# Two bias additions move from GpSimd instructions to accumulating transfers that GpSimd issues

## The chip, the cores and the metric

The kernel runs on one core of one Trainium2 chip. The metric is the device time of one execution in microseconds (us), where less is better. The engines are named as the profile names them: PE is the matrix engine (PEld is its loading of weights), DVE the vector engine, ACT the scalar engine, POOL GpSimd, and SP the engine whose queue issues most transfers between DRAM and the on-chip memory.

## The reference, cut to what matters

```python
x = layernorm(x + attn(x))        # linear attention, 16 heads
x = layernorm(x + xattn(x, ctx))  # channel attention, two variants added, 4 heads
x = layernorm(x + ffn(x))         # one expert of 8 for each batch

def attn(x):
    q, k, v = split(x @ Wqkv.T + bqkv)
    q, k = elu(q * scale) + 1, elu(k * scale) + 1
    y = q * cumsum(k * v) / max(sum(q * cumsum(k)), 0.001)
    return y @ Wproj.T + bproj                 # bproj: 512 numbers

def ffn(x):
    e = argmax(x.mean(1) @ Wr + br)            # for each batch
    return relu(x @ W1[e] + b1[e]) @ W2[e] + b2[e]   # b2[e]: 512 numbers
```

x and ctx are 16 batches of 512 tokens by 512 channels in fp32. The change touches how the two biases at the ends of these functions, `bproj` and `b2[e]`, come into x.

## The kernel before, in words

Every matrix product is done three times with operands split into a high part (rounded to fp32r) and a low part (the rest): high by high, high by low, low by high. ACT rounds (`wq`, `xT_hi`, `we_hi`, `h_hi`), DVE subtracts to get the low part (`xT_lo`, `we_lo`, `h_lo`).

The kernel is a software pipeline written out by hand. An outer loop runs over i = 0 to 19, an inner one over h = 0 to 31. In step i five stages work on five batches: a = i (attention), c = i-1 (channel attention), e = i-2 (second normalisation and choice of the expert), b = i-3 (the expert's two products) and z = i-4 (third normalisation and the store). In each h, a function `mix(i, h)` of each engine emits what the stages a, c, e and z have at this h; between these pieces stand the products of the expert's layers, `up` at even h and `down` at odd h. The four compute engines and SP have one program each, in this order, and meet at semaphores (`dve.wait_ge(proj_mm, ...)`). An engine runs its own instructions in order, so what stands behind a waiting instruction waits with it.

Names that are needed below:

- `X[n]`, n = 0 to 3, are four buffers of 128 partitions by 4x512 fp32 (1 MB). Batch a is in `X[a % 4]` from its load (`x_tok`, SP, at h = 15) to its store four steps later. Everything is added to it in place.
- POOL adds `bproj` to `X[a]` (L338 in the kernel before) after the load has landed (`xtok_in`), from a copy of the bias on all partitions, `rows[:, BPROJ]`. It signals `xb_done`. DVE's `residual1(a, t)` (L643) waits for that and for the projection's product, at h = 24 to 27.
- POOL adds `b2` to `X[b]` (L320) at the head of step i, after PE has transposed x (`tr_mm`), from a small tile `b2` that SP has loaded for the chosen expert (L254). It signals `b2_done`; DVE's `residual3(z, t)` (L658) waits for it one step later, at h = 1.
- Behind L320 on POOL stands `diagonal(c_col)` (L311), which PE's `ctx_sums` (L951) needs at h = 5. Behind L338 stands `diagonal(k_all2)` (L311), which waits for DVE (`kall2_done`, L735) and which PE's `constants` (L992) needs at h = 21.
- DVE's `weigh(c, v)` at h = 16 and 17 turns the exponentials into weights (`junk_v` L722, `a_v` L726, their sum L738). PE's `attention_T` (L985) transposes the sum at h = 19. DVE's `denominator(a)` at h = 18 (L605 to L611) leads over ACT (`rden_all`, L506) to PE's `spread_reciprocal` (L916) at h = 20.
- SP loads the expert's weights into two buffers `raw` (L260), each as soon as DVE has made the low part of the chunk two before (`wlo_done`, L760); ACT rounds a chunk at L424. It loads the projection weights `wq` for q, k and v again in each step (L191) into three buffers.

Of the kernel before, what the change touches and what calls it, by code (L numbers as in the profile page):

```python
# [7 lines left out]
ALU = mybir.AluOpType  # L8
# [3 lines left out]
P = 128  # L12
NB = 16
T = 512
C = 512
CC = C // P
TT = T // P
# [5 lines left out]
NE = 8  # L23
# [11 lines left out]
NX = 4  # L35
# [17 lines left out]
def build(nc, d, out):  # L53
    wq_dram = nc.dram_tensor("wq_scratch", [JOBS, P, 2 * CC * P], F32, kind="Internal").ap()

    with ExitStack() as ctx:
        def sb(name, shape, dt=F32):
            return ctx.enter_context(nc.sbuf_tensor(name, shape, dt))

        def sem(name):  # L60
            return ctx.enter_context(nc.semaphore(name))
# [18 lines left out]
        ctx_T = sb("ctx_T", [P, CC, T])  # L80
        e_f, r_f = sb("e_f", [P, T]), sb("r_f", [P, T])
        k_sum, kv_sum, q = sb("k_sum", [P, T]), sb("kv_sum", [P, T]), sb("q", [P, T])
        rows = sb("rows", [P, 9, C])
        WKG, BKG, WKL, BKL, WVG, BVG, WVL, BVL, BPROJ = range(9)
        c_sb = sb("c_sb", [P, XH, P])
        diag = sb("diag", [P, XH, P])
        s_a, a_v = sb("s_a", [P, 2, XH, P]), sb("a_v", [P, 2, XH, P])
        aT = sb("aT", [P, XH, P])
        const_b = sb("const_b", [P, C])
        x_sum = sb("x_sum", [P, C])  # L90
        b2 = sb("b2", [P, 1, C])

        ident, ones = sb("ident", [P, P]), sb("ones", [P, P])
        head_sum = sb("head_sum", [P, CC, SEG])
# [64 lines left out]
            sem(n) for n in ("mean_mm", "mcol_done", "route_mm", "logit_done", "top_done", "found_done", "idx_done"))  # L159
        tr_mm, x2hi_done, x2lo_done = sem("tr_mm"), sem("x2hi_done"), sem("x2lo_done")  # L160
        we_in = [sem(f"we_in{s}") for s in range(NR)]
        b1_in, b2_in = [sem("b1_in0"), sem("b1_in1")], sem("b2_in")
        whi_done, wlo_done = sem("whi_done"), sem("wlo_done")
        up_mm, h_done, hhi_done, hlo_done, down_mm, acc_mm = (
            sem(n) for n in ("up_mm", "h_done", "hhi_done", "hlo_done", "down_mm", "acc_mm"))
        b2_done, res3_done, stored = sem("b2_done"), sem("res3_done"), sem("stored")
        JOB_MM = (k_mm, v_mm, q_mm)

        block = ctx.enter_context(nc.Block())
# [5 lines left out]
        def _(sp):  # L175
# [21 lines left out]
            sp.dma_start(b_qkv[:, :], d["b_qkv"]).then_inc(small_in, 16)  # L197
            sp.dma_start(scale[:, :], d["scale"].broadcast_to([P, 1])).then_inc(small_in, 16)
            load_raw(3)
            sp.dma_start(rows[:, :, :], d["rows"].broadcast_to([P, 9, C])).then_inc(consts_in, 16)  # L200
            sp.dma_start(wr[:, :, :], d["wr"]).then_inc(consts_in, 16)
            sp.dma_start(br[:, :], d["br"]).then_inc(consts_in, 16)
            sp.dma_start(X[NX - 1][:, :, :].rearrange("p t n -> p (t n)"), d["w_proj"]).then_inc(wp_in, 16)
# [1 line left out]
            for i in range(NB + 4):  # L205
                a, c, e, b, z = stages(i)
                for h in range(HALVES):
                    if h in JOB_AT:
                        j = JOB_AT.index(h)
                        if i == 0:  # L210
                            store_job(j)
                            if j + 4 < JOBS:
                                load_raw(j + 4)
                        if i > 0 and inside(a) and j + NQ < JOBS:
                            load_job(a, j + NQ)
                        if inside(a + 1) and j + NQ >= JOBS:
                            load_job(a + 1, j + NQ - JOBS)
                    if h == 11 and inside(z):
                        sp.wait_ge(norm_done, TT * z + TT)
                        sp.dma_start(out[z], X[z % NX][:, :, :]).then_inc(stored, 16)  # L220
                    if h == 15 and inside(a):

                        if (due := upto(z, 16, 16)) is not None:
                            sp.wait_ge(stored, due)
                        if a == NX - 1:
                            sp.wait_ge(wplo_done, 1)
                        sp.dma_start(X[a % NX][:, :, :], d["x_tok"][a]).then_inc(xtok_in, 16)
                    if h == 18 and inside(a + 1):

                        sp.wait_ge(den_mm, a + 1)  # L230
                        sp.dma_start(xT_raw[:, :, :], d["xT"][a + 1]).then_inc(xT_in, 16)
                    if h == 23 and inside(a):

                        sp.wait_ge(yhi_done, CC * a + CC)
                        sp.wait_ge(ylo_done, CC * a + CC)
                        sp.dma_start(ctx_tok[:, :, :], d["ctx_tok"][a]).then_inc(ctx_in, 16)
                    if h == 26 and inside(a):

                        if (due := upto(c, TT, TT)) is not None:
                            sp.wait_ge(out_mm, due)  # L240
                        if (due := upto(c, XH, XH)) is not None:
                            sp.wait_ge(csum_done, due)
                        sp.dma_start(ctx_T[:, :, :], d["ctxT"][a]).then_inc(ctxT_in, 16)
                    if h == 26 and inside(e):
                        sp.wait_ge(idx_done, e + 1)
                        expert = sp.value_load(idx[0:1, e:e + 1], min_val=0, max_val=NE - 1)

                        if (due := upto(e - 2, FC, FC)) is not None:
                            sp.wait_ge(h_done, due)
                        sp.dma_start(b1[:, e % 2, :], d["b1"][bass.ds(expert, 1)].rearrange("a p f -> p (a f)")).then_inc(b1_in[e % 2], 16)  # L250

                        if (due := upto(e - 1, 1, 1)) is not None:
                            sp.wait_ge(b2_done, due)
                        sp.dma_start(b2[:, 0, :], d["b2"][bass.ds(expert, 1), :].broadcast_to([P, C])).then_inc(b2_in, 16)  # L254
                    g = FC * b + h // 2 + 3
                    if h % 2 == 1 and 0 <= g < NB * FC:

                        if g >= NR:
                            sp.wait_ge(wlo_done, g - NR + 1)
                        sp.dma_start(raw[:, g % NR, :],  # L260
                                     d["w12"][bass.ds(expert, 1), g % FC].rearrange("a p n -> p (a n)")).then_inc(we_in[g % NR], 16)
# [3 lines left out]
        def _(pool):  # L265
# [48 lines left out]
            for i in range(NB + 4):  # L314
                a, c, e, b, z = stages(i)
                if inside(b):

                    pool.wait_ge(tr_mm, CC * b + CC)
                    pool.wait_ge(b2_in, 16 * b + 16)
                    pool.tensor_tensor(X[b % NX][:, :, :], X[b % NX][:, :, :],  # L320
                                       b2[:, 0:1, :].broadcast_to([P, TT, C]), ALU.add).then_inc(b2_done, 1)
                if inside(c):
                    pool.wait_ge(csum_done, XH * c + XH)

# [10 lines left out]
                    rstd_of(2, z)  # L335
                if inside(a):
                    pool.wait_ge(xtok_in, 16 * a + 16)
                    pool.tensor_tensor(X[a % NX][:, :, :], X[a % NX][:, :, :],  # L338
                                       rows[:, BPROJ:BPROJ + 1, :].broadcast_to([P, TT, C]), ALU.add).then_inc(xb_done, 1)
                if inside(c):  # L340
                    pool.wait_ge(kall2_done, c + 1)

# [204 lines left out]
        def _(dve):  # L547
# [90 lines left out]

            def residual1(a, t):
                dve.wait_ge(proj_mm, TT * a + t + 1)  # L640
                dve.wait_ge(xb_done, a + 1)
                x = X[a % NX][:, t, :]
                dve.tensor_tensor(x, AB[(t + 1) % 2][:, :], x, ALU.add).then_inc(res1_done, 1)  # L643

# [6 lines left out]
            def residual3(z, t):  # L651
                if t < TT - 1:
                    dve.wait_ge(acc_mm, (TT - 1) * z + t + 1)
                else:
                    dve.wait_ge(down_mm, FC * z + FC)
                dve.wait_ge(b2_done, z + 1)
                x = X[z % NX][:, t, :]
                dve.tensor_tensor(x, acc[t][:, :], x, ALU.add).then_inc(res3_done, 1)  # L658

# [495 lines left out]
```

## Time and profile before

| | us |
|---|---|
| median of 3 runs | 2568.96 (2568.95 to 2569.8) |
| the profiled execution, its own time | 2571.94 |
| its span, first to last instruction | 2570.2 |
| PE busy | 2430.1 (95% of the span) |
| DVE busy | 1747.5 (68%) |
| ACT busy | 1172.2 (46%) |
| POOL busy | 533.6 (21%) |
| transfers, share of 16 DMA engines | 37.4% |

The times are device times; the profile is one more execution, in which every instruction is recorded. A line of the profile names the line of the kernel, the engine, the operation, what is written and what is read, and for an engine that stood idle in front of the instruction, what released it. "Issue" stands where the profile shows nothing that was waited for.

### The profile page before, as it was taken

Reading aid. Unit: us, or ns where it says so; the run is one execution under the profiler, and the core shown is the slowest. Engines: PE = TensorE matmul, PEld = TensorE weight load, DVE = VectorE, ACT = ScalarE, POOL = GpSimd, SP = SyncE. Lnnn points to the kernel's source line nnn. Section 1 sums busy time; section 2 is a strip of 40 time slices with the busy share of each in tenths; the row PEclk is TensorE's granted clock in tenths of the full one; section 3 lists DMA queues with packets and bytes.
Section 4 is the critical chain, followed back from the end, with each engine's and each line's share of the span. In section 5 each row is a group of like instructions: output and inputs, shape, how many; then the busy total and the mean of one; then the engine's idle time right before and its main releaser. Section 6 shows DMA issues by size and latency. Waiting matters only on the chain.

```text
span 2570.2 us, 33240 instructions
## 1 busy us (share of the span) xinstructions
PE 2430.1 (95%) x11584; PEld 1988.8 (77%) x11584; DVE 1747.5 (68%) x2721; ACT 1172.2 (46%) x1920; POOL 533.6 (21%) x452
## 2 busy tenths in 40 slices
PE   6866899999999999999999999999999999999998
PEld 5655688878788787878878787887878888877876
DVE  6567576677767677676767768667776767765443
ACT  4223444545444443554544455454545445354543
POOL 3132212122112212221122122212212221222110
PEclk9877899999999999999999999999999999999999
DMA  7333333433434344343433434343343434222332
GB/s 274 113 109 107 127 141 117 140 136 108 172 103 159 116 139 145 106 156 119 156 119 121 150 124 160 112 146 128 115 158 117 156 114 145 95 82 87 115 108 69
DMA packets 83400, 331.85 MB, mean 129 GB/s; under 512 B 11810, under 2 KB 11810, under 8 KB 72738
## 3 DMA queue, kind: packets, MB, share of 16 engines
q1 hardware_dynamic: 83234, 329.72, 37.4%
q8 instruction: 94, 1.54, 0.2%
q14 instruction: 72, 0.59, 0.1%
HBM read 306.61 MB, written 23.07 MB: 128 GB/s over the span
## 4 chain that ended last, share of the span: by engine, by line
PE 81%; DVE 10%; ACT 4%; issue 3%; DMA 1%; POOL 1%; SPq 0%; ACTq 0%; DVEq 0%; POOLq 0%
PE m L868 25%; PE acc L1045 24%; PE h_ps L868 23%; DVE junk_v L722 3%; PE m L1003 2%; PE m L944 2%; DVE a_v L726 2%; ACT const_b L465 1%; PE m L1019 1%; PE m L916 1%; PE m L951 1%; DVE h_lo L768 1%; POOL diag L311 1%; PE m L992 1%; ACT rden_all L506 1%
## 5 line engine op out<-in xcount | busy, mean ns | idle before, releaser
L868 PE MATMUL m<-xT_hi,wq 128*128 128x512 f32 x1536 | 514.2, 399 | 24.8 <-DVE wq L550 10.7
L424 ACT ACTIVATE we_hi<-raw 128x1024 fp32r<-128x1024 f32 x256 | 270.7, 1058 | 505.4 <-PE acc L1045 500.3
L760 DVE TENSOR_TENSOR we_lo<-raw,we_hi 128x1024 fp32r<-128x1024 f32 x256 | 368.7, 1440 | 177.6 <-ACT we_hi L424 177.6
L1045 PE MATMUL acc<-we_hi,h_hi 128*128 128x512 f32 x1024 | 423.3, 413 | 0.4
L868 PE MATMUL h_ps<-x2T_hi,we_hi 128*128 128x512 f32 x1024 | 403.4, 394 | 6.0 <-DVE x2T_lo L754 6.0
L1045 PE MATMUL acc<-we_hi,h_lo 128*128 128x512 f32 x1024 | 400.8, 391 | 0.0
L1045 PE MATMUL acc<-we_lo,h_hi 128*128 128x512 f32 x1024 | 400.5, 391 | 0.0
L868 PE MATMUL h_ps<-x2T_lo,we_hi 128*128 128x512 f32 x1024 | 399.6, 390 | 0.0
L868 PE MATMUL h_ps<-x2T_hi,we_lo 128*128 128x512 f32 x1024 | 399.6, 390 | 0.0
L434 ACT ACTIVATE hid<-h_ps,b 128x512 f32<-128x512 f32 x256 | 175.7, 686 | 458.5 <-PE h_ps L868 458.5
L868 PEld LDWEIGHTS m<-xT_hi,wq 128*128 128x128 f32 x1536 | 295.2, 192 | 91.1 <-issue 28.0
L768 DVE TENSOR_TENSOR h_lo<-hid,h_hi 128x512 fp32r<-128x512 f32 x256 | 182.9, 714 | 253.1 <-ACT h_hi L439 252.9
L868 PE MATMUL m<-xT_lo,wq 128*128 128x512 f32 x768 | 304.3, 396 | 0.0
L1045 PEld LDWEIGHTS acc<-we_hi,h_hi 128*128 128x128 f32 x1024 | 193.4, 189 | 49.1 <-issue 9.6
L868 PEld LDWEIGHTS h_ps<-x2T_hi,we_hi 128*128 128x128 f32 x1024 | 192.7, 188 | 45.7 <-DVE x2T_lo L754 6.7
L1045 PEld LDWEIGHTS acc<-we_lo,h_hi 128*128 128x128 f32 x1024 | 193.5, 189 | 43.4 <-issue 7.0
L1045 PEld LDWEIGHTS acc<-we_hi,h_lo 128*128 128x128 f32 x1024 | 192.9, 188 | 42.3
L868 PEld LDWEIGHTS h_ps<-x2T_hi,we_lo 128*128 128x128 f32 x1024 | 192.8, 188 | 40.4
L868 PEld LDWEIGHTS h_ps<-x2T_lo,we_hi 128*128 128x128 f32 x1024 | 192.9, 188 | 38.6
L381 ACT ACTIVATE e_f<-m,sb_qkv,scale 128x512 f32<-128x512 f32 x128 | 99.9, 780 | 220.8 <-PE m L868 217.5
L338 POOL TENSOR_TENSOR x<-x,rows 128x2048 f32<-128x2048 f32 x16 | 74.1, 4629 | 544.4 <-DMA x<-in_x_tok 544.4
L868 PEld LDWEIGHTS m<-xT_lo,wq 128*128 128x128 f32 x768 | 147.9, 193 | 31.3 <-issue 1.0
(126 smaller groups left out, 3480.4 us busy)
## 6 DMA issues: line engine op xcount, KB each, us to landing
raw<-in_w SPq DMA_DIRECT2D x256, 512.0 KB, 3.8
wq<-wq_scratch SPq DMA_DIRECT2D x180, 512.0 KB, 3.3
xT_raw<-in_xT SPq DMA_DIRECT2D x16, 1024.0 KB, 5.9
x<-in_x_tok SPq DMA_DIRECT2D x16, 1024.0 KB, 5.4
ctx_tok<-in_ctx_tok SPq DMA_DIRECT2D x16, 1024.0 KB, 4.9
ctx_T<-in_ctxT SPq DMA_DIRECT2D x16, 1024.0 KB, 4.9
out_dram<-x SPq DMA_DIRECT2D x16, 1024.0 KB, 4.8
wq_scratch<-wq SPq DMA_DIRECT2D x12, 512.0 KB, 4.5
```

The costliest lines, as they stand in the source:

```text
L338: pool.tensor_tensor(X[a % NX][:, :, :], X[a % NX][:, :, :], rows[:, BPROJ:BPROJ + 1, :].broadcast_to([P, TT, C]), ALU.add).then_inc(xb_do ...
L381: act.activation(e_f[:, :], ps[:, :], ACT.Exp, bias=sb_qkv[:, col:col + 1], scale=scale[:, 0:1]).then_inc(done, 1)
L424: act.activation(we_hi[:, g % NW, :], raw[:, g % NR, :], ACT.Copy).then_inc(whi_done, 1)
L434: act.activation(hid[:, f % 2, :], H_PS[:, :], ACT.Relu, bias=b1[:, b % 2, f:f + 1]).then_inc(h_done, 1)
L722: dve.scalar_tensor_tensor(junk_v[:, h % 2, :], s_a[:, v, h, :], e_rec2[:, v, h:h + 1], rows[:, bv, h * P:h * P + P], ALU.mult, ALU.mult, ...
L726: dve.scalar_tensor_tensor(a_v[:, v, h, :], s_a[:, v, h, :], e_rec2[:, v, h:h + 1], rows[:, wv, h * P:h * P + P], ALU.mult, ALU.mult).then ...
L760: dve.tensor_tensor(we_lo[:, g % NW, :], raw[:, g % NR, :], we_hi[:, g % NW, :].bitcast(F32), ALU.subtract).then_inc(wlo_done, 1)
L768: dve.tensor_tensor(h_lo[:, f % 2, :], hid[:, f % 2, :], h_hi[:, f % 2, :].bitcast(F32), ALU.subtract).then_inc(hlo_done, 1)
L868: last = pe.matmul(out, lhsT, rhs, start=(n == 0), stop=(n == 3 * len(pairs) - 1))
L944: last = pe.matmul(by_head[:, h, :], X[c % NX][:, t, hs], ctx_tok[:, t, hs], start=(t == 0), stop=(t == TT - 1))
L1003: last = pe.matmul(M2[:, h * P:h * P + P], ctx_T[:, h, t * P:t * P + P], aT[:, h, :], start=True, stop=True)
L1045: last = pe.matmul(acc[t][:, :], hx[:, f % 2, ts], wx[:, g % NW, C:], start=(f == 0 and n == 0), stop=(f == FC - 1 and n == 2))
```

## The change

Both additions leave POOL's arithmetic. In their place POOL issues a transfer from DRAM into `X` that adds what it brings to what is there (`accum_op=ALU.add`). The source is a row of 512 numbers in DRAM, read again for each of 128 partitions and 4 token groups; the destination is the whole 1 MB buffer. Since the row of `b2` depends on the expert, POOL now reads the index itself. The tile `b2`, its load by SP, its semaphore `b2_in` and the ninth row of `rows` go. `b2_done` becomes two semaphores, used in turn, and `xb_done` counts 16 for each batch.

```diff
@@ sp
-                        if (due := upto(e - 1, 1, 1)) is not None:
-                            sp.wait_ge(b2_done, due)
-                        sp.dma_start(b2[:, 0, :], d["b2"][bass.ds(expert, 1), :].broadcast_to([P, C])).then_inc(b2_in, 16)
@@ pool
                 if inside(b):
 
+                    pool.wait_ge(idx_done, b + 1)
+                    expert = pool.value_load(idx[0:1, b:b + 1], min_val=0, max_val=NE - 1)
                     pool.wait_ge(tr_mm, CC * b + CC)
-                    pool.wait_ge(b2_in, 16 * b + 16)
-                    pool.tensor_tensor(X[b % NX][:, :, :], X[b % NX][:, :, :],
-                                       b2[:, 0:1, :].broadcast_to([P, TT, C]), ALU.add).then_inc(b2_done, 1)
+                    pool.dma_start(X[b % NX][:, :, :], d["b2"][bass.ds(expert, 1), :].unsqueeze(1).broadcast_to([P, TT, C]),
+                                   accum_op=ALU.add).then_inc(b2_done[b % 2], 16)
...
                 if inside(a):
                     pool.wait_ge(xtok_in, 16 * a + 16)
-                    pool.tensor_tensor(X[a % NX][:, :, :], X[a % NX][:, :, :],
-                                       rows[:, BPROJ:BPROJ + 1, :].broadcast_to([P, TT, C]), ALU.add).then_inc(xb_done, 1)
+                    pool.dma_start(X[a % NX][:, :, :], d["b_proj"].broadcast_to([P, TT, C]), accum_op=ALU.add).then_inc(xb_done, 16)
@@ dve
             def residual1(a, t):
                 dve.wait_ge(proj_mm, TT * a + t + 1)
-                dve.wait_ge(xb_done, a + 1)
+                dve.wait_ge(xb_done, 16 * a + 16)
...
-                dve.wait_ge(b2_done, z + 1)
+                dve.wait_ge(b2_done[z % 2], 16 * (z // 2) + 16)
```

On POOL, this is one step of the kernel before, from the addition of `b2` (L320) to the one of `bproj` (L338) and the diagonal behind it:

```order
L320 TENSOR_TENSOR x3<-x3,b2 128x2048 [waits b2_in,tr_mm]
L311 TENSOR_TENSOR diag<-ident,c_col 128x512 [waits kb_mm,csum_done]
L305 TENSOR_TENSOR x_sum<-x0 128x512 [waits sx_mm,x2_done]
L308 TENSOR_TENSOR x_sum<-x_sum,x0 128x512 [waits x2sum_done] x2
L295 TENSOR_TENSOR var_e<-mv,ln_eps 128x4 [waits norm_done,mv2_done]
...
L338 TENSOR_TENSOR x2<-x2,rows 128x2048 [waits xtok_in]
L311 TENSOR_TENSOR diag<-ident,k_all2 128x512 [waits c_mm,kall2_done]
```

The same stretch of POOL in the changed kernel (its line numbers are four or five lower) is this:

```order
L314 TENSOR_LOAD idx [waits idx_done]
L314 ISA x2
L316 ISA [waits tr_mm]
L316 DMA x<-in_b 128x4x512
L306 TENSOR_TENSOR diag<-ident,c_col 128x512 [waits kb_mm,csum_done]
L300 TENSOR_TENSOR x_sum<-x 128x512 [waits sx_mm,x2_done]
L303 TENSOR_TENSOR x_sum<-x_sum,x 128x512 [waits x2sum_done] x2
L290 TENSOR_TENSOR var_e<-mv,ln_eps 128x4 [waits norm_done,mv2_done]
...
L334 DMA x<-in_b_proj 128x4x512 [waits xtok_in]
L306 TENSOR_TENSOR diag<-ident,k_all 128x512 [waits c_mm,kall2_done]
```

Nothing has changed places: each addition is replaced where it stood, and the first one has the reading of the index in front of it. DVE, ACT and PE keep their instructions and their order; on SP only the load of `b2` is gone.

## Rows read from the trace of the kernel before

**Rows 1.** The page: the busy time of the engines and its share of the span.
```profile
PE 2430.1 (95%) x11584; PEld 1988.8 (77%) x11584; DVE 1747.5 (68%) x2721; ACT 1172.2 (46%) x1920; POOL 533.6 (21%) x452
```
**Rows 2.** Busy time in a stretch: length, PE, PEld, DVE, ACT, POOL, clock, DMA share, GB/s.
```profile
304.00:1131.00 827.00, 813.20 (x3927) 667.92 (x3927) 590.12 (x913) 396.63 (x659) 167.73 (x135) 1.00 0.39 134
```
**Rows 3.** Waits of PE over the run: us in total, times, the longest.
```profile
PE m L868 <- issue: 23.9, 15, 1.6
PE m L985 <- DVE a_v L738: 21.0, 14, 7.7
PE m L916 <- ACT rden_all L506: 11.6, 3, 6.2
```
**Rows 4.** Instructions of DVE's line L722: ns min/median/max, first and last start.
```profile
L722 DVE SCALAR_TENSOR_TENSOR junk_v<-s_a,e_rec,rows x128: 345/349/4744, 136.1 to 2324.8; 128x128 f32<-128x128 f32 x128
```
**Rows 5.** POOL in order of time in one middle step: start, duration, idle before.
```profile
1197.92 5.05 POOL L320 TENSOR_TENSOR x<-x,b 128x2048 f32<-128x2048 f32 x1
1227.09 1.04 POOL L311 TENSOR_TENSOR diag<-ident,c_col 128x512 f32<-128x512 f32 x1 [24.11 <-ACT const_b L465]
...
1281.14 4.59 POOL L338 TENSOR_TENSOR x<-x,rows 128x2048 f32<-128x2048 f32 x1 [34.77 <-DMA x<-in_x_tok]
1290.33 1.08 POOL L311 TENSOR_TENSOR diag<-ident,k_all 128x512 f32<-128x512 f32 x1 [4.60 <-DVE k_all L735]
```
**Rows 6.** DVE in order of time in the same step.
```profile
1199.03 5.03 DVE L760 TENSOR_TENSOR we_lo<-raw,we_hi 128x1024 fp32r<-128x1024 f32 x1
...
1281.23 4.65 DVE L722 SCALAR_TENSOR_TENSOR junk_v<-s_a,e_rec,rows 128x128 f32<-128x128 f32 x1
...
1291.60 0.69 DVE L738 TENSOR_TENSOR a_v<-a_v 128x512 f32<-128x512 f32 x1
...
1314.16 0.67 DVE L643 TENSOR_TENSOR x<-m,x 128x512 f32<-128x512 f32 x1
```
**Rows 7.** PE in order of time around the transposes of h = 19.
```profile
1291.07 0.39 PE L868 MATMUL h_ps<-x2T_hi,we_lo 128*128 128x512 f32 x1
1292.34 0.66 PE L985 MATMUL m<-ident,a_v 128*128 128x128 f32 x4 [0.88 <-DVE a_v L738]
...
1295.42 0.39 PE L1045 MATMUL acc<-we_lo,h_hi 128*128 128x512 f32 x1
1295.65 0.39 PE L1045 MATMUL acc<-we_hi,h_lo 128*128 128x512 f32 x1
1296.12 0.73 PE L916 MATMUL m<-rden_all,head_all 128*128 128x512 f32 x2
...
1299.88 1.02 PE L992 MATMUL m<-diag,ones 128*128 128x512 f32 x2
```
**Rows 8.** DVE and PE in order of time in the steps i = 1 and 2.
```profile
138.45 4.25 DVE L713 TENSOR_TENSOR e_rec<-e_rec,wp 128x4 f32<-128x4 f32 x1
...
146.68 1.11 PE L985 MATMUL m<-ident,a_v 128*128 128x128 f32 x4 [7.74 <-DVE a_v L738]
...
242.33 3.22 DVE L609 CAST den<-rden 128x128 fp32r<-128x128 f32 x1
...
248.00 1.22 PE L916 MATMUL m<-rden_all,head_all 128*128 128x512 f32 x2 [6.18 <-ACT rden_all L506]
```
**Rows 9.** POOL and DVE in order of time in step i = 0.
```profile
59.55 4.55 POOL L338 TENSOR_TENSOR x<-x,rows 128x2048 f32<-128x2048 f32 x1 [40.36 <-DMA x<-in_x_tok]
...
71.80 0.69 DVE L643 TENSOR_TENSOR x<-m,x 128x512 f32<-128x512 f32 x1 [5.34 <-PE m L868]
```
**Rows 10.** Transfers by kind (KB each, median us to landing), and SP and ACT in time.
```profile
raw<-in_w SPq DMA_DIRECT2D x256, 512.0 KB, 3.8
...
x<-in_x_tok SPq DMA_DIRECT2D x16, 1024.0 KB, 5.4
...
1296.03 3.55 SPq L260 DMA_DIRECT2D raw<-in_w  x2
...
1303.77 1.06 ACT L424 ACTIVATE we_hi<-raw 128x1024 fp32r<-128x1024 f32 x1 [1.26 <-PE acc L1045]
```

More of the change, by code:

```diff
@@ L82, in build @@
         k_sum, kv_sum, q = sb("k_sum", [P, T]), sb("kv_sum", [P, T]), sb("q", [P, T])
-        rows = sb("rows", [P, 9, C])
-        WKG, BKG, WKL, BKL, WVG, BVG, WVL, BVL, BPROJ = range(9)
+        rows = sb("rows", [P, 8, C])
+        WKG, BKG, WKL, BKL, WVG, BVG, WVL, BVL = range(8)
         c_sb = sb("c_sb", [P, XH, P])
@@ L90, in build @@
         x_sum = sb("x_sum", [P, C])
-        b2 = sb("b2", [P, 1, C])
         ident, ones = sb("ident", [P, P]), sb("ones", [P, P])
@@ L161, in build @@
         we_in = [sem(f"we_in{s}") for s in range(NR)]
-        b1_in, b2_in = [sem("b1_in0"), sem("b1_in1")], sem("b2_in")
+        b1_in = [sem("b1_in0"), sem("b1_in1")]
         whi_done, wlo_done = sem("whi_done"), sem("wlo_done")
@@ L165, in build @@
             sem(n) for n in ("up_mm", "h_done", "hhi_done", "hlo_done", "down_mm", "acc_mm"))
-        b2_done, res3_done, stored = sem("b2_done"), sem("res3_done"), sem("stored")
+        b2_done, res3_done, stored = [sem("b2_done0"), sem("b2_done1")], sem("res3_done"), sem("stored")
         JOB_MM = (k_mm, v_mm, q_mm)
@@ L199, in _ @@
             load_raw(3)
-            sp.dma_start(rows[:, :, :], d["rows"].broadcast_to([P, 9, C])).then_inc(consts_in, 16)
+            sp.dma_start(rows[:, :, :], d["rows"].broadcast_to([P, 8, C])).then_inc(consts_in, 16)
             sp.dma_start(wr[:, :, :], d["wr"]).then_inc(consts_in, 16)
@@ L1134 @@
         "scale": g["L0_attn_scale"].reshape(1, 1),
-        "rows": np.stack([x_names[n] for n in ("wkg", "bkg", "wkl", "bkl", "wvg", "bvg", "wvl", "bvl")]
-                         + [g["L0_attn_bproj"]])[None],
+        "rows": np.stack([x_names[n] for n in ("wkg", "bkg", "wkl", "bkl", "wvg", "bvg", "wvl", "bvl")])[None],
+        "b_proj": g["L0_attn_bproj"].reshape(1, 1, C),
         "cols": np.stack([column(x_names[n]) for n in ("wqg", "bqg", "wql", "bql", "wp", "bp")], axis=1),
```

## The prediction

> **What bounds the kernel now.** I read the page first, then the busy time by stretches, the waits of PE, and one middle step in order of time on POOL, DVE and PE. The page says PE: busy for 2430.1 us, 95% of the span [rows 1]. From 304 to 1131 us PE is busy for 813.2 of 827 us at full clock [rows 2]: 13.8 us, 1.7%, are without work. So nothing that merely relieves POOL or DVE can bring more than that in the middle of the run, and only where PE's wait ends on the relieved work. The waits of PE name the places [rows 3]: the transposes L985 wait for DVE's a_v for 21.0 us in 14 waits, the first spreading product L916 for 11.6 us, and a third group, ahead of the projection, for 23.9 us in 15.
>
> POOL is busy for 21% of the span and stands idle ahead of most of its work [rows 1, 5], so its own time is worth nothing. What its additions do to DVE is the point. While L338 runs (1281.14 to 1285.73), DVE's L722 takes 4.65 us from 1281.23 to 1285.88; the median of this line is 0.349 us [rows 4 to 6]. It ends when POOL's instruction ends. The same stands at the other addition: L320 runs from 1197.92 to 1202.97, and DVE's we_lo takes 5.03 us beside it [rows 5, 6]. So a big addition on POOL holds up a DVE instruction with two on-chip inputs for its whole length. In steps a = 3 to 14 it is each time the weighing of the attention (I counted 12), and behind it come the sum L738 and the transposes on PE.
>
> **The change part by part.**
>
> *The addition of bproj leaves POOL.* DVE gets 4.65 - 0.35 = 4.3 us back in each middle step. PE uses only what it waits for. The last product before the transposes starts at 1291.07; products follow each other every 0.23 us (1295.42, 1295.65), so the transposes could start at 1291.30 and start at 1292.34: 1.04 us lost. The product L916 could start at 1295.88 and starts at 1296.12: 0.24 us [rows 7]. Both waits end on DVE's chain, which now comes 4.3 us earlier, that is 3.3 and 3.0 us before PE asks. Together 1.28 us a step, twelve times: 15.4 us.
>
> In step 1 DVE's L713, an instruction of four columns, takes 4.25 us beside the addition, against some 0.16 us for such a row elsewhere, and PE waits for 7.74 us on what follows [rows 8]. The whole 4.1 us comes back. In step 2 the held instruction is the cast L609, 3.22 us where its others take 0.23, and PE waits for 6.18 us on rden_all behind it [rows 8]: 3.0 us. As a check, the group of L985 has 21.0 us [rows 3]: 12 x 0.88 in the middle and 7.74 in step 1 leave 2.7, which is step 2's, where a_v was made before the addition began and the wait stays; of the 11.6 us of L916 6.18 are step 2's. The third group, 1.6 us a step ahead of the projection, I count as staying: the addition of const_b (L350), which is not changed, holds DVE there in the same way.
>
> Gain so far: 15.4 + 4.1 + 3.0 = 22.5 us.
>
> *The addition of b2 leaves POOL.* DVE's we_lo gets 3.8 us back, but no wait of PE ends on it: the three groups of [rows 3] stand elsewhere, and PE has other products between h = 0 and 4. Nothing gained. POOL reads the index and issues; the next thing on its queue, the diagonal at 1227.09, sits idle for 24.11 us on ACT [rows 5], so this costs nothing up to that length. The sum in X is wanted by residual3 a step later, over 150 us: the transfer is covered whatever it takes. SP loses one load a step, off the path.
>
> *The transfer that adds bproj, issue.* The trace shows no transfer issued by POOL. Below, SP's issues return within half a microsecond; above, the addition itself, 4.6 us. I take 2 us. Behind it on POOL waits the diagonal of k_all, which ran at 1290.33 to 1291.41 while PE's L992 starts at 1299.88 [rows 5, 7]. With PE 1.3 us earlier POOL may be busy until 1297.5, so an issue of up to 16 us costs nothing.
>
> *The same, landing.* This is the unknown that matters. The nearest row is the plain load of the same megabyte, 5.4 us from issue to landing [rows 10]. An adding transfer must also read the destination: twice, 10.8 us, is my value. As bounds I take 5.4 us and 25 us (POOL's 4.6 us as issue, and four times a load's time, since the row doesn't say what 512 pieces of 2 KB in place of 128 of 8 KB cost). The deadline is residual1: in the middle steps L643 starts at 1314.16, 33.0 us after POOL was free to begin [rows 5, 6]; in steps 1 and 2 it is 28 and 24 us by the same two lines; in step 0 it is 71.80 - 59.55 = 12.25 us [rows 9]. With 10.8 us all hold, step 0 by little, and there the path of its first use is new. I charge 1 us for step 0.
>
> *The same, beside other transfers.* The engines for transfers are in use for 39% of the time [rows 2]. Of the loads that run within 15 us of the issue, the one that is needed soonest is raw at 1296.03, landing 3.8 us later and rounded by ACT at 1303.77 [rows 10]: 3.9 us to spare, as much again as the load itself takes. The load before it was issued only once the held DVE had made its low part, and comes 4 us earlier now. So sharing costs nothing unless the adding transfer is still running at 1296, 15 us after its issue.
>
> Two rules of the Trainium skill, SBUF — State Buffer, section Who interferes with whom, bear on the unseen issue. A DVE instruction with two inputs in SBUF contends with a GpSimd instruction that reads SBUF, not with one that only writes it; by this, writing descriptors would not hold DVE, and all of the 4.3 us returns. Against the change, the same section says that the making of descriptors starves while DVE is in a two-port mode. Whether the cast and the scalar maximum of the denominator run so no row tells; they are 0.23 and 0.28 us long, so by it the transfer starts half a microsecond later at most, and the sum stays. No run here shows either for a transfer.
>
> As an estimate from the formula of DMA: Bandwidth & Descriptors, section Anatomy of one DMA, about 2 us plus the bytes over 436 GB/s, a plain megabyte takes 4.4 us, and with the read counted as well 6.8 us; the rows' 5.4 us for the plain load are the firmer ground.
>
> **The sum.** -22.5 + 1 = -21.5 us. On the profiled execution's own time, 2571.94 us (span 2570.2), that gives 2550.4; on the median of the runs, 3.0 us less than this execution, 2547.5 us, 0.84% faster.
>
> **The rivals.**
>
> *The transfer lands late (slower).* Place: residual1 waits for xb_done, DVE's queue stands, and the two PSUM banks of the projection are not freed. Each us beyond 12 costs step 0 a us, beyond about 21 step 2, beyond 24 step 1, beyond 31.7 (33.0 less PE's gain) all middle steps. At 26 us the cost is 14 + 5 + 2 = 21 us: break even. At 36 us it is 24 + 15 + 12 + 12 x 4.3 = 103, less 22.5: 2649 us. For it: an addition in a transfer is unseen, and each partition's row is read back in 2 KB pieces. Against it: it would have to take five to seven times a plain load. Chance 0.12.
>
> *The middle case, 14 to 24 us.* Step 0 loses 2 to 12 us, and raw at 1296 loses its margin in some steps, up to 0.5 us a step. Gain 5 to 18: 2551 to 2564, say 2556 us. Chance 0.15.
>
> *The issue holds DVE as the addition did.* If POOL's issue lasts and blocks like L338, DVE gets nothing back: 2568 to 2572 us. The hold must be over 3.0 us to cost anything of the middle steps, and 4.3 to cost all. For it: both are work of POOL on the on-chip memory. Against it: the source comes from DRAM, and POOL reads no tile. Chance 0.10.
>
> *More than forecast.* With DVE ahead, the wait before the projection goes as well, 15 x 1.6 = 24 us more: 2524 us. Against it: it hangs on L350, which moves along with PE. Chance 0.03.
>
> **How the numbers follow.** Forecast 0.60, with a range of its own of 2542 to 2554 (from the middle steps alone, 15.4 us, to the full 22.5 and 4 us more in the first 300 us, where PE's clock isn't steadily granted). With the middle case, 0.75; to leave out no more than 2 in 10, the range goes on to the no-change case: 2541 to 2567. A measurement of this kernel tells 0.2%, 5 us, from no change. Faster: 0.60 + 0.03 + 0.13 of the middle case = 0.76. Same: 0.10 + 0.02 = 0.12. Slower: 0.12.
>
> **What the profile of after would show.** Right: no L722, L713 or L609 over 1 us; the group PE m L985 waiting for a_v gone; each middle step of PE 1.3 us shorter; the group ahead of the projection still 1.6 us a step; DVE's we_lo at the head of a step near 1.2 us. The issue on POOL shows as a row or as a gap ahead of the diagonal. Wrong: DVE's x (L638 there) with idle time ended by the transfer x<-in_b_proj, in step 0 first; DVE rows of 4 us beside POOL's issue; ACT's we_hi waiting for raw; or a landing beyond 25 us.

## The result, and the profile after

The changed kernel takes 2537.89 us (median of four runs, 2537.43 to 2539.95), the kernel before 2569.17 us in the same session (2568.95 to 2569.80). The ratio is 0.9878, 95% interval 0.9866 to 0.9890: 1.22%, 31.3 us, faster. The forecast was 2547.5 us, with a range of 2541 to 2567, so the gain was 10 us larger than forecast and 3 us outside the range. The profiled execution took 2537.97 us, its span is 2536.3 us. That is 33.9 us less than the span before, and the accounts below are of these 33.9 us.

The page of after, engines and transfers (KB each, median us from issue to landing):
```profile
PE 2417.4 (95%) x11584; PEld 1987.2 (78%) x11584; DVE 1631.3 (64%) x2721; ACT 1171.4 (46%) x1920; POOL 423.6 (17%) x452
...
q0 software_dynamic: 16896, 33.56, 8.6%
...
raw<-in_w SPq DMA_DIRECT2D x256, 512.0 KB, 4.2
...
x<-in_b_proj POOLq DMA_DIRECT2D x16, 1024.0 KB, 12.2
...
x<-in_b POOLq DMA_DIRECT2D x16, 1024.0 KB, 11.6
```
Two stretches of after, with the columns of [rows 2]:
```profile
304.00:1131.00 827.00, 818.33 (x3991) 675.48 (x3990) 560.84 (x945) 397.05 (x660) 135.58 (x138) 1.00 0.48 149
200.00:230.00 30.00, 23.10 (x115) 18.66 (x115) 24.65 (x42) 11.26 (x29) 4.54 (x3) 0.96 0.46 158
```
and the second of them in the kernel before:
```profile
200.00:230.00 30.00, 25.40 (x104) 19.97 (x105) 22.40 (x36) 8.86 (x21) 5.71 (x4) 0.83 0.32 105
```
In 827 us PE now runs 3991 products in place of 3927 [rows 2], and 8.7 us are without work in place of 13.8. The second stretch shows something else: the granted clock is 0.96 there and was 0.83, and PE finishes eleven products more in a shorter busy time.

The waits of PE after, which answer to [rows 3]:
```profile
PE m L863 <- issue: 23.9, 15, 1.6
...
PE m L911 <- ACT rden_all L501: 7.9, 3, 3.4
PE m L1014 <- DVE x2T_lo L749: 7.7, 1, 7.7
...
PE m L980 <- DVE a_v L733: 6.6, 2, 3.7
```
The group ahead of the projection is the same to the tenth. The transposes wait in steps 1 and 2 alone; the twelve middle waits are gone. One middle step, as in [rows 5 to 7], POOL first:
```profile
1260.35 1.35 POOL L334 DMA_DIRECT2D x<-in_b_proj  x1 [35.52 <-DMA x<-in_x_tok]
1264.50 1.07 POOL L306 TENSOR_TENSOR diag<-ident,k_all 128x512 f32<-128x512 f32 x1 [2.80 <-DVE k_all L730]
```
DVE:
```profile
1261.02 1.22 DVE L755 TENSOR_TENSOR we_lo<-raw,we_hi 128x1024 fp32r<-128x1024 f32 x1
...
1265.75 0.69 DVE L733 TENSOR_TENSOR a_v<-a_v 128x512 f32<-128x512 f32 x1
1266.36 0.68 DVE L763 TENSOR_TENSOR h_lo<-hid,h_hi 128x512 fp32r<-128x512 f32 x1
```
PE:
```profile
1269.53 0.39 PE L863 MATMUL h_ps<-x2T_hi,we_lo 128*128 128x512 f32 x1
1269.76 0.60 PE L980 MATMUL m<-ident,a_v 128*128 128x128 f32 x4
1270.12 0.48 PE L1040 MATMUL acc<-we_hi,h_hi 128*128 128x512 f32 x1
...
1272.74 0.39 PE L1040 MATMUL acc<-we_hi,h_lo 128*128 128x512 f32 x1
1272.97 0.61 PE L911 MATMUL m<-rden_all,head_all 128*128 128x512 f32 x2
```
and every instruction of the line that was held (min, median, max in ns; [rows 4] had a maximum of 4744):
```profile
L717 DVE SCALAR_TENSOR_TENSOR junk_v<-s_a,e_rec,rows x128: 345/348/354, 135.9 to 2290.9; 128x128 f32<-128x128 f32 x128
```
The issue takes POOL 1.35 us. DVE's we_lo starts in the middle of it and takes its usual 1.22 us, so the issue holds nothing here. The diagonal behind it reads SBUF and does hold the weighing a little: from 1264.33 two weighings take 1.39 us in place of 0.61, which costs PE nothing. The sum a_v ends at 1266.44, and PE takes it up at 1269.76, 0.23 us behind the product before. Read by starts, and not by the printed idle time, the transposes lost 1.04 us before and lose nothing now.

**Where the 33.9 us come from.** The 11584 products stand in the same order in both kernels, so each can be set against its counterpart. PE is ahead by 4.3 us at the counterpart of 147 us, 6.9 at 230, 4.9 at 241, 8.5 at 248, 9.4 at 270, 11.6 at 286, 11.1 at 300, 31.9 at 2261 and 33.9 at the end. So: 11.1 us in the first 300 us, 20.8 in the twelve middle steps (1.73 each), 2.0 in the drain. There PE runs two groups of some twenty products at the lower level of its clock before (granted clock 0.72 from 2262 to 2268 us, 0.76 from 2465 to 2472) and one such group after (0.72 from 2340 to 2346), and nothing in the traces ties these 2 us to the change.

### The profile page after: what moved, and what is told of

The parts are those of the page before. It is cut to its first block, busy times and chain, and to the rows that moved or that the text cites. A ratio compares the mean times of both kernels' runs of the same rounds, so it can differ in the third digit from the quotient of the medians.

```text
span 2536.3 us, 33258 instructions
## 1 busy us (share of the span) xinstructions
PE 2417.4 (95%) x11584; PEld 1987.2 (78%) x11584; DVE 1631.3 (64%) x2721; ACT 1171.4 (46%) x1920; POOL 423.6 (17%) x452
## 4 chain that ended last, share of the span: by engine, by line
PE 89%; DVE 3%; ACT 3%; issue 3%; POOL 1%; DMA 1%; ACTq 0%; DVEq 0%; POOLq 0%; SPq 0%
PE acc L1040 28%; PE h_ps L863 26%; PE m L863 25%; PE m L998 2%; PE m L939 2%; ACT const_b L460 1%; PE m L898 1%; PE m L1014 1%; PE m L946 1%; PE m L911 1%; POOL diag L306 1%; PE m L987 1%; ACT r_f L377 1%; PE m L964 0%; PE m L953 0%
## 5 line engine op out<-in xcount | busy, mean ns | idle before, releaser
L755 DVE TENSOR_TENSOR we_lo<-raw,we_hi 128x1024 fp32r<-128x1024 f32 x256 | 313.8, 1226 | 175.5 <-ACT we_hi L419 175.5
L434 ACT ACTIVATE h_hi<-hid 128x512 fp32r<-128x512 f32 x256 | 161.9, 632 | 8.1
## 6 DMA issues: line engine op xcount, KB each, us to landing
x<-in_b_proj POOLq DMA_DIRECT2D x16, 1024.0 KB, 12.2
x<-in_b POOLq DMA_DIRECT2D x16, 1024.0 KB, 11.6
```

What stands on the lines that cost most here:

```text
L434: act.activation(h_hi[:, f % 2, :], hid[:, f % 2, :], ACT.Copy).then_inc(hhi_done, 1)
L755: dve.tensor_tensor(we_lo[:, g % NW, :], raw[:, g % NR, :], we_hi[:, g % NW, :].bitcast(F32), ALU.subtract).then_inc(wlo_done, 1)
```

## The experiments

Eleven more kernels were run; the kernel before had medians of 2567.8 to 2569.0 us beside them. "A step" is a middle step, and its gain is read from the same alignment of PE's products. Line numbers shift by a few lines from kernel to kernel.

**1. Each half of the change alone.** `bproj_only` makes the bproj edit and leaves b2 on GpSimd; `b2_only` makes the other.
```diff
 bproj_only
-  pool.tensor_tensor(X[a % NX][:, :, :], X[a % NX][:, :, :], rows[:, BPROJ:BPROJ + 1, :]..., ALU.add).then_inc(xb_done, 1)
+  pool.dma_start(X[a % NX][:, :, :], d["b_proj"].broadcast_to([P, TT, C]), accum_op=ALU.add).then_inc(xb_done, 16)
 b2_only
-  pool.tensor_tensor(X[b % NX][:, :, :], X[b % NX][:, :, :], b2[:, 0:1, :]..., ALU.add).then_inc(b2_done, 1)
+  pool.dma_start(X[b % NX][:, :, :], d["b2"][bass.ds(expert, 1), :]..., accum_op=ALU.add).then_inc(b2_done[b % 2], 16)
```


> Only bproj goes by an adding transfer; b2 stays a POOL addition. Theory (the gain is DVE's, freed in the weighing of the attention, with h_lo queued behind it): the middle steps fall from 152.0 to 150.3 us as with both changes, steps 1 and 2 give their 8.5 us, and the 2.2 us that PE waits less for the first expert's weights (in front of the first steps of stage b) are missing: 2569.2 - 20.8 - 9 = about 2539 to 2541. Rival (each of the two freed DVE instructions is worth the same): half of the 31 us, about 2553.

> Only b2 goes by an adding transfer. Theory: DVE's we_lo at the head of a step is short again but nothing on PE ends on it, the middle steps stay at 152.0 us; only SP's queue, which no longer loads b2 ahead of the first expert's first weights, gives about 2 us once: 2567. Rival (each freed DVE instruction counts the same): about 2553.

`bproj_only`: 2541.45 us, ratio 0.9892 (0.9877 to 0.9907); 1.75 us a step. `b2_only`: 2565.41 us, ratio 0.9985 (0.9976 to 0.9994); 0.00 us a step, and the wait for a_v is all there:
```profile
PE m L982 <- DVE a_v L735: 26.0, 14, 7.7
```
Both came within 2 us of what was expected, and far from the rival's 2553. The whole gain of the middle steps belongs to bproj. What b2 brings comes once, between 284 and 300 us, 1.5 us in the trace.

**2. Where b2's microseconds come from.** At the start of the expert stage SP's queue in the kernel before holds the load of b2 ahead of the first weights. SP and ACT, before:
```profile
272.64 0.34 SPq L254 DMA_DIRECT2D b<-in_b  x1
273.17 9.93 SPq L260 DMA_DIRECT2D raw<-in_w  x3
...
280.28 1.06 ACT L424 ACTIVATE we_hi<-raw 128x1024 fp32r<-128x1024 f32 x1 [4.72 <-DMA raw<-in_w]
```
SP and ACT, after:
```profile
263.21 8.03 SPq L255 DMA_DIRECT2D raw<-in_w  x3
...
268.43 1.06 ACT L419 ACTIVATE we_hi<-raw 128x1024 fp32r<-128x1024 f32 x1 [2.31 <-DMA raw<-in_w]
```
From SP's first issue of raw to ACT's use it was 7.1 us and is 5.2, and PE gains 2.17 us at its next wait. `b2_load_later` is the kernel before with b2's load moved behind the first two of these loads:
```diff
+                    if h == 30 and inside(e):
                         if (due := upto(e - 1, 1, 1)) is not None:
                             sp.wait_ge(b2_done, due)
                         sp.dma_start(b2[:, 0, :], ...).then_inc(b2_in, 16)
```


> The kernel before, with one edit: SP issues the load of b2 two places later, behind the first of the expert's weights, POOL's additions unchanged. Theory: this load, issued right in front, delays the first raw, for which ACT and behind it the transposes of PE at 285 us wait; the 2.2 us come back without any adding transfer: 2567, middle steps 152.0. Rival (the 2.2 us come from DVE or POOL being freer): no change, 2569.

2565.50 us, ratio 0.9988 (0.9979 to 0.9997), nothing in the middle steps. ACT in this kernel, where SP issues the first load of raw at 271.61:
```profile
276.65 1.06 ACT L424 ACTIVATE we_hi<-raw 128x1024 fp32r<-128x1024 f32 x1 [2.12 <-DMA raw<-in_w]
279.05 2.93 ACT L396 ACTIVATE x<-x,shift,rstd 128x512 f32<-128x512 f32 x4 [1.35 <-POOL shift L301]
```
ACT takes the first weights up 5.0 us after the issue, as in the changed kernel (5.2), so the place in the queue accounts for this whole delay. PE gets only a part of it: its wait is 8.8 us long, between the 9.9 of before and the 7.7 of after, because ACT's next instruction now waits 1.35 us for POOL, a wait that the late weights covered before. By their medians `b2_load_later` and `b2_only` can't be told apart (2565.50 and 2565.41 us). The medians say little here, since executions differ in their first 300 us by more than the 2 us in question: `h_lo_first` below, whose program differs from before only from step 3 on, is 5.5 us ahead at 300 us.

**3. The hold by itself.** Two kernels put a GpSimd instruction that reads SBUF behind the new issue (a sum of two blocks of `rows` into an unused tile), a third one that only writes.
```diff
 hold_read_4us (the changed kernel, and)
+  pool.tensor_tensor(spare[:, :, :], rows[:, 0:4, :], rows[:, 4:8, :], ALU.add).then_inc(spare_done, 1)
 hold_read_2us
+  pool.tensor_tensor(spare[:, 0:2, :], rows[:, 0:2, :], rows[:, 4:6, :], ALU.add).then_inc(spare_done, 1)
 no_read_6us (three times)
+  pool.memset(spare[:, :, :], 0.0).then_inc(spare_done, 1)
```


> The changed kernel, with one POOL addition of 128x2048 of two on-chip tiles into a spare tile right behind the issue of the bproj transfer (4.6 us, result not used). Theory (a POOL instruction that reads the on-chip memory holds a two-input DVE instruction for its length): one DVE instruction of the weighing takes some 4.6 us again, L980 waits again and the middle steps go back to 151.8 to 152.5 us: 2562 to 2572. Rival (the wait was for the addition's result or POOL's queue): 2538.

> As before it, but the spare addition is 128x1024, about 2.3 us. Theory: DVE's chain is 3.3 us ahead of PE's transposes and about 3 us ahead of the product behind them, so a hold of 2 us in the same place costs nothing: 2537 to 2540, though DVE shows it. Rival (each us of hold costs its share, 31 us over 4.3 us): about 2553.

> As before it, but instead of an addition POOL writes the spare tile three times (memset of 128x2048, about 2 us each), reading nothing. Theory (only reading holds DVE): DVE's rows keep their short times, 2537 to 2540. Rival (any use of the on-chip memory by POOL holds DVE): L980 waits, 2565 to 2580.

`no_read_6us`: 2539.02 us, ratio 0.9894 (0.9880 to 0.9908). Six microseconds of GpSimd work stand there, and DVE's weighing beside it keeps its pace (each instruction 0.35 us):
```profile
1259.79 6.08 POOL L339 MEMSET spare<- 128x2048 f32 x3
...
1262.28 0.35 DVE L726 SCALAR_TENSOR_TENSOR a_v<-s_a,e_rec,rows 128x128 f32<-128x128 f32 x1
...
1263.60 0.69 DVE L738 TENSOR_TENSOR a_v<-a_v 128x512 f32<-128x512 f32 x1
```
The cast of the denominators (L609), which has one input, isn't free beside the memset: it takes 1.89 and 1.24 us in steps 1 and 2, against 0.23 in the changed kernel, and PE's wait for rden_all in step 2 is 3.1 us long in place of 2.1. In the middle steps no memset meets it.

`hold_read_4us`: 2586.49 us, ratio 1.0074 (1.0061 to 1.0087), expected 2562 to 2572: the hold is there as expected, but it costs more than the addition of before did. POOL and DVE:
```profile
1292.24 1.35 POOL L335 DMA_DIRECT2D x<-in_b_proj  x1 [35.69 <-DMA x<-in_x_tok]
1293.10 5.08 POOL L339 TENSOR_TENSOR spare<-rows 128x2048 f32<-128x2048 f32 x1
...
1291.68 6.66 DVE L726 SCALAR_TENSOR_TENSOR a_v<-s_a,e_rec,rows 128x128 f32<-128x128 f32 x4
```
Four weighings take 6.66 us; in the changed kernel four take 1.14. The hold is thus 5.5 us, and it stands later than before, ahead of we_lo too. A step is 2.96 us longer than after: 1.74 of it is everything that the change had won, 0.85 a new wait of PE for we_lo (0.08 more go into slower products behind it), the rest the transposes that come later still.

`hold_read_2us`: 2553.48 us, ratio 0.9943 (0.9930 to 0.9956). I had expected 2537 to 2540, since I took the added instruction to last 2.3 us, below the 3.0 to 3.3 us by which DVE's chain is early. A miss. The time is the rival's (about 2553), but by luck: it was summed for a hold of some 2 us, and with the 3.4 us of hold that the rows show, its 31 us over 4.3 us would give about 2562. POOL, DVE and PE:
```profile
1273.54 1.35 POOL L335 DMA_DIRECT2D x<-in_b_proj  x1 [33.86 <-DMA x<-in_x_tok]
1274.40 2.88 POOL L339 TENSOR_TENSOR spare<-rows 128x1024 f32<-128x1024 f32 x1
...
1273.19 4.25 DVE L726 SCALAR_TENSOR_TENSOR a_v<-s_a,e_rec,rows 128x128 f32<-128x128 f32 x3
...
1282.97 0.68 DVE L768 TENSOR_TENSOR h_lo<-hid,h_hi 128x512 fp32r<-128x512 f32 x1
...
1283.11 0.66 PE L985 MATMUL m<-ident,a_v 128*128 128x128 f32 x4
1283.80 0.47 PE L1045 MATMUL acc<-we_hi,h_hi 128*128 128x512 f32 x1
```
Three weighings take 4.25 us in place of 0.86: 3.4 us of hold beside a 2.9 us instruction. The transposes come 0.12 us late, and the product into acc 0.28 us more, since h_lo, which DVE makes behind the sum, ends only at 1283.65. The product L916 loses 0.25 us, and 0.17 us are slower products right behind these waits. Altogether 0.82 us a step, 9.8 us in the twelve middle steps; the other 8.2 us by which this execution trails the changed kernel at its end arise in the first 300 us.

**4. Is it h_lo?** Before, acc starts 0.70 us behind the transposes of [rows 7]; after, 0.36. DVE and PE in the kernel before:
```profile
1292.20 0.68 DVE L768 TENSOR_TENSOR h_lo<-hid,h_hi 128x512 fp32r<-128x512 f32 x1
...
1293.04 0.47 PE L1045 MATMUL acc<-we_hi,h_hi 128*128 128x512 f32 x1
```
Either acc waits for h_lo, which stands on DVE's queue behind the held weighing, or PE is slow to start again after a wait. `h_lo_first` is the kernel before with h_lo moved ahead of the second weighing.
```diff
                 for h in range(HALVES):
+                    if h == 17 and inside(b):
+                        hidden(b, h // 2)
                     mix(i, h)
 ...
-                    if h % 2 == 1 and inside(b):
+                    if h % 2 == 1 and h != 17 and inside(b):
                         hidden(b, h // 2)
```


> The kernel before, with one VectorE instruction moved: the low part of the hidden values (h_lo, 0.6 to 0.7 us) of this half step stands ahead of the second weighing instead of behind the sum a_v. Asked: why the product into acc starts 0.70 us behind the transposes of a_v in the kernel before and 0.35 us in the changed one. The sum a_v, and TensorE's transposes that wait for it, come about 0.6 us later (wait 1.65 instead of 1.04 us in each of 12 middle steps) in both theories. Theory 1 (acc waits for h_lo, which is queued behind the held weighing): the distance from the transposes to acc falls to 0.36 to 0.42 us, the step is 152.3 us long, the time 2570 to 2574. Theory 2 (TensorE's next weights are not preloaded while it waits, whatever VectorE does): the distance stays at 0.70 us, the step is 152.6 us long, the time 2574 to 2578.

2569.05 us, ratio 1.0004 (0.9994 to 1.0013). PE:
```profile
1287.71 0.66 PE L987 MATMUL m<-ident,a_v 128*128 128x128 f32 x4 [1.53 <-DVE a_v L738]
1288.12 0.48 PE L1047 MATMUL acc<-we_hi,h_hi 128*128 128x512 f32 x1
```
The transposes still wait, and the distance falls to 0.41 us: acc did wait for h_lo. My time was too high (2570 to 2574, step 152.3 against a measured 152.0) because I forgot that DVE's denominators move up into the place that h_lo leaves: L916 gains back 0.33 us and the step comes out even.

**5. The addition kept on GpSimd, but later.** `bproj_late_on_pool` moves the addition of before behind those of const_b, past the weighing.
```diff
-                if inside(a):                        (ahead of the diagonals)
-                    pool.wait_ge(xtok_in, 16 * a + 16)
-                    pool.tensor_tensor(X[a % NX]..., rows[:, BPROJ:BPROJ + 1, :]..., ALU.add).then_inc(xb_done, 1)
...
+                if inside(a):                        (behind the additions of const_b)
+                    pool.wait_ge(xtok_in, 16 * a + 16)
+                    pool.tensor_tensor(X[a % NX]..., rows[:, BPROJ:BPROJ + 1, :]..., ALU.add).then_inc(xb_done, 1)
```


> The kernel before, with bproj still added by POOL, but behind the additions of const_b instead of in front of the diagonal of k_all: no adding transfers at all. Theory (what counts is where DVE is held, not that POOL does the work): PE no longer waits at the transposes, but residual1 is due at about 1.5 us after the addition ends (1308.25 + 4.6 against 1314.2, less the gain), so 0 to 1.5 us a step are lost there: 2540 to 2560. Rival (the gain needs the work to leave POOL): 2569 or more.

2588.15 us, ratio 1.0077 (1.0063 to 1.0090): slower than before, where my theory had it faster (2540 to 2560). The time lies in the rival's open range (2569 or more), but not for the rival's reason, that the work must leave POOL. POOL, DVE and PE:
```profile
1310.81 5.02 POOL L349 TENSOR_TENSOR x<-x,rows 128x2048 f32<-128x2048 f32 x1
...
1311.32 5.60 DVE L761 TENSOR_TENSOR we_lo<-raw,we_hi 128x1024 fp32r<-128x1024 f32 x1
1316.84 0.68 DVE L650 TENSOR_TENSOR x<-m,x 128x512 f32<-128x512 f32 x1
...
1317.57 0.60 PE L1004 MATMUL m<-aT,ctx_T 128*128 128x128 f32 x3 [3.07 <-DVE x L650]
```
The wait for a_v is gone in the middle steps, as meant, and the 1.74 us of the changed kernel are won there. The hold now meets we_lo, behind which residual2 stands, and the PSUM bank that residual2 should free keeps PE waiting for 3.07 us; by starts this place loses 3.4 us a step, and more in the first ones. The addition was not removed but moved to a place where less slack was left.

**6. The transfer twice.** `transfer_twice` issues the transfer of bproj a second time once the first has landed, so the bias is added twice; xb_done comes with the second.
```diff
+  pool.dma_start(X[a % NX][:, :, :], d["b_proj"]..., accum_op=ALU.add).then_inc(xb_half, 16)
+  pool.wait_ge(xb_half, 16 * a + 16)
   pool.dma_start(X[a % NX][:, :, :], d["b_proj"]..., accum_op=ALU.add).then_inc(xb_done, 16)
```


> The changed kernel with the bproj transfer done twice, the second issued when the first has landed (the bias is added twice, so the output is another one). The sum of the two landings is about 24.5 us. Theory: step 0 has room for 12.2 us and loses about 12; step 2 has about 20 and loses up to 4; the middle steps have 31 and lose nothing unless the weights' loads beside the second transfer run out of their 1 to 5 us of margin: 2550 to 2556. Rival (the transfers' share of the engines already costs the middle steps): middle steps clearly over 150.3 us, 2560 and more.

2556.07 us, ratio 0.9950 (0.9938 to 0.9962), at the upper end of what was expected. DVE in step 0, and PE's waits:
```profile
85.38 0.69 DVE L641 TENSOR_TENSOR x<-m,x 128x512 f32<-128x512 f32 x1 [19.42 <-DMA x<-in_b_proj]
...
PE m L866 <- DVE x L641: 12.6, 1, 12.6
PE m L990 <- POOL diag L307: 10.6, 4, 4.9
```
Step 0 loses about 15 us and the middle steps nothing (1.90 us a step ahead of before). DVE waits for the transfer in the first step alone. Steps 1 and 2 lose something else: there PE waits 4.9 and 4.6 us for the diagonal, which stands on POOL behind the new wait for the first landing. Over the first 300 us this execution falls 22.7 us behind the changed kernel, and not only the 15 of step 0.

**7. The third group.** PE's remaining wait, 1.6 us ahead of the projection, was put down in the prediction to the additions of const_b. `const_b_later` is the changed kernel with one more wait ahead of them; `const_b_later_alone` is the kernel before with the same.
```diff
+                    if inside(a):
+                        pool.wait_ge(ylo_done, CC * a + CC)
                     for t in range(TT):
                         pool.tensor_tensor(X[c % NX][:, t, :], X[c % NX][:, t, :], const_b[:, :], ALU.add).then_inc(x1c_done, 1)
```


> The changed kernel, and in it GpSimd additionally waits for all of VectorE's low parts of the context (ylo_done) before its additions of k_all2 to const_b. In both kernels these additions read SBUF while VectorE splits x for the projection, and TensorE then waits about 1.6 us a step ahead of the projection (the group with 15 waits, the same before and after the change). Main theory (a two-input VectorE instruction is held for as long as a GpSimd instruction that reads SBUF runs): the group of 15 goes, since nothing on GpSimd reads SBUF at that point; const_b is needed only for residual2 some 15 us later. 1.6 us in 12 to 15 steps: 2514 to 2521 us, ratio to before about 0.980. Rival A: the additions are now so late that they hold we_lo or residual2, as in the run with the projection bias added late on GpSimd; then the gain at the projection is given back there, and the time is 2530 to 2550. Rival B: the wait ahead of the projection belongs to something other than the hold (ScalarE's high part): no change against the changed kernel, 2536 to 2541.

> The kernel before (both biases added by GpSimd instructions), with the one wait of const_b_later: GpSimd's additions of const_b wait for all of VectorE's low parts of the context. Asked: whether the gain of 1.79 us a step ahead of the projection is independent of the change, as it must be if each hold is a local matter of which VectorE instruction runs beside which GpSimd read. Main theory: the sum is additive. The trace shows 1.75 to 1.85 us a middle step gained at the first product of the projection (15 steps), the wait for a_v stays at 1.04 us; 2539 to 2545 us, ratio 0.989 to 0.991. Rival: the additions of the two biases and of const_b are a chain on GpSimd, so that a later const_b delays the next additions and the wait for a_v grows; then under 1 us a step is left, 2550 to 2565 us.

`const_b_later`: 2507.66 us (2503.59 to 2513.21), ratio 0.9760 (0.9743 to 0.9777), 61 us or 2.4% faster than before and the best version found. DVE's two xT_lo in the changed kernel:
```profile
1282.10 3.42 DVE L616 TENSOR_TENSOR xT_lo<-ctx_tok,xT_hi 128x512 fp32r<-128x512 f32 x2 [2.44 <-ACT xT_hi L396]
```
and here, with POOL and PE, and the stretch of [rows 2]:
```profile
1268.68 1.29 DVE L618 TENSOR_TENSOR xT_lo<-ctx_tok,xT_hi 128x512 fp32r<-128x512 f32 x2 [2.43 <-ACT xT_hi L398]
...
1270.15 6.31 POOL L347 TENSOR_TENSOR x<-x,const_b 128x512 f32<-128x512 f32 x4 [17.99 <-DVE xT_lo L618]
...
1270.44 0.39 PE L865 MATMUL m<-wp_hi,xT_hi 128*128 128x512 f32 x1
...
304.00:1131.00 827.00, 826.54 (x4037) 683.71 (x4037) 562.80 (x955) 399.25 (x662) 141.95 (x139) 1.00 0.48 150
```
2.13 us of hold are gone, the projection follows without a gap, and PE is busy for 826.5 of 827 us. A step gains 1.79 us more, which over the fifteen steps of this group makes 26.9 us, the difference of the spans. The median fell by 30 us and below my range (2514 to 2521): I had used the printed idle time, 1.6 us, where the starts of the products say 1.77. With the 26.9 us the median would be 2511; the last 3 us lie within the spread of its own five runs. `const_b_later_alone`: 2537.22 us, ratio 0.9879 (0.9863 to 0.9896), 1.77 us a step at the projection, and the wait for a_v untouched. The two edits gain 31.3 and 31.0 us alone and 60.8 together: the holds are local, as expected.

## Why the prediction was right, and where it failed

- **The hold as the mechanism: right.** The held instructions are at their usual length, `bproj_only` carries the middle steps, and of the two GpSimd instructions tried behind the issue only the reading one brings the weighing's hold back. The rule of the Trainium skill, SBUF — State Buffer, section Who interferes with whom, that a two-input DVE instruction contends with a GpSimd instruction that reads SBUF and not with one that only writes, was borne out on both sides: 3.4 and 5.5 us of hold beside reads, none of the weighing beside 6 us of memset or beside the 1.35 us issue. The rule against the change (starved descriptors) showed nothing: the transfer of this step was issued in 1.35 us, and all 16 landed within 13.9 us.
- **The size.** The sum said 21.5 us on the profiled execution, and the span fell by 33.9. Of the missing 12.4 us, 5.4 are the middle steps, 5.0 the first 300 us (11.1 against 22.5 - 15.4 - 1 = 6.1) and 2.0 the drain, for which the sum had nothing.
- **"Together 1.28 us a step": the first step that failed, a term too small.** Measured 1.73. The missing 0.45 us are 0.28 us of acc, which waited for h_lo behind the same held instruction (`h_lo_first`, `hold_read_2us`), and 0.06 and 0.11 us by which the transposes and the products of L916 ran slower right after a wait; the 1.04 and 0.24 came out within 0.02. Over twelve steps 5.4 us. I had followed the two waits that the list names and not gone on down DVE's queue from the held instruction: h_lo ended at 1292.88 and acc started at 1293.04, with no wait printed between.
- **"SP loses one load a step, off the path": the second.** True of the middle steps. At the start of the expert stage, where the first weights are awaited, it was on the path once: 2.2 us at PE's wait in the whole change, 1.5 us in `b2_only` by 300 us, 0.9 in `b2_load_later`.
- **The first 300 us: 11.1 us against 6.1.** Step 1 gave 4.0 and L916 of step 2 gave 3.7 (predicted 4.1 and 3.0). The load gave 2.2, and some 0.9 came between 248 and 270 us. Some 3 us more are PE's clock between 200 and 230 us, 0.96 in place of 0.83, which is PE at 2.4 GHz for products that ran at 1.2 GHz before; about 2 of them went back into the waits up to 241 us. What sets this clock stays open. PE gains nothing in this stretch in `b2_only`, `b2_load_later` and the two hold_read, which hold DVE near the weighing, and 3.0 us in `bproj_only` and `transfer_twice`, which don't; but it gains 4.4 in `const_b_later_alone` and 1.6 in `h_lo_first`, which hold it too, and nothing in `const_b_later` and `bproj_late_on_pool`, which don't. Each kernel gives one profiled execution.
- **Step 2: the mechanism right, the place luck.** That the addition met the cast L609 is particular to the profiled execution of before. In the other traces in which POOL keeps this addition at its old place (`b2_only`, `b2_load_later`, `h_lo_first`, `const_b_later_alone`) it comes 3.5 to 14 us earlier and holds DVE's work at or just behind the weighing; PE then waits 7.6 to 9.2 us for a_v and 2.1 for rden_all, in place of 2.5 and 6.2. The changed kernel waits 2.9 and 2.1. Counted by these two waits the change is worth 3.8 us in step 2 against before and 4.8 to 6.3 against the other four; the forecast 3.0 were read off one case.
- **Landing and issue: right.** 12.2 us (10.8 taken), 1.35 us (2 taken). Step 0, charged 1 us, lost nothing, and that by little: issued at 59.5, landed at 71.3, used at 71.5. In `bproj_only`, `no_read_6us` and `hold_read_2us` it is this transfer that ends DVE's wait there.
- **Sharing: right in time, thin in margin.** The load of raw issued at 1262.40, beside the new transfer, took 8.9 us to land; a comparable one before took 3.6. ACT took it up 2.0 us after landing, in the tightest step 1.0 us. No wait came of it. It was the load before the one that the prediction had priced as the tightest (3.9 us to spare).
- **The third group stays: right,** for the reason given. The rival in which it goes needs an edit of its own, and `const_b_later` is that edit.
- **"The hold must be over 3.0 us to cost anything": not contradicted, and not tested closely.** Holds of 0.8 us (the diagonal) cost nothing and holds of 3.4 us cost 0.82 us a step; none in between was tried at this place. And it can't be read as the length of GpSimd's instruction: one of 2.9 us held DVE for 3.4.

## What to carry to other kernels

When one held instruction is set free, walk down its engine's queue and price every consumer behind it, by the starts of the waiting engine's instructions rather than by the printed idle time; the list of waits had 0.88 us where the starts say 1.04, and nothing where acc lost 0.28. Before replacing work on GpSimd, see whether it reads SBUF beside a two-input DVE instruction that is on the path: one wait that moves the read to a quiet place was worth as much as the transfer (31 us each), and a wrong place made the kernel 19 us slower than before. Look at the first step of a loop by itself, since the slack for a transfer and the queue of loads are different there.

## What the hardware showed that I had not expected

- A hold by a reading GpSimd instruction that follows an issue is longer than the instruction: 5.5 us beside 5.1, 3.4 beside 2.9. By the records the held DVE instruction could have ended before the read began (the third weighing would have been done near 1274.1, the read starts at 1274.40). It is so in every middle step of both kernels: the held instruction starts 0.5 to 0.8 us ahead of the read's record and ends 0.16 us behind it. Whether POOL's records start late or the read takes its hold earlier isn't told by these rows.
- An accumulating transfer of 1 MB in 512 rows of 2 KB lands in 10.8 to 13.9 us, against a median of 5.4 us for a plain load of the same size. The 32 of them are 8.6% of the transfer engines' time, and the load of 512 KB issued 2 to 3 us behind one in each middle step lands in 8.3 to 9.9 us, against the 3.6 of the comparable one before.
